# Routing of three chunks placed between attention heads, and the second attention placed between the last gate products

## The reference

```
x += tanh(g_xattn[0]) * MHA16(layernorm(x), ctx)      # 16 heads of 8 features, softmax over 256 keys
x += tanh(g_ffn[0])   * refine(layernorm(x))          # "experts of a controller", below
x += tanh(g_xattn[1]) * softmax(ln(x) @ ctx.T) @ ctx  # one head over 128 features
x += tanh(g_ffn[1])   * MoE(layernorm(x))             # top 2 of 8 experts, silu(x W1 + b1)*(x W2 + b2) W3 + b3

refine(y): top 2 of 8 experts by a router (gelu hidden layer of 32), their softmax weights w
   twice:  for the shared net and the two chosen experts k:
             a, b, g = split(gelu([s, v] @ W1 + b1) @ W2 + b2)
             v_k = sigmoid(a) * v - softplus(b) * (s - mu);  s_k = s + 0.1 * sigmoid(g) * v_k
           s, v move by halt = sigmoid(...) toward the weighted mean of s_k, v_k
   out = y + integration_weight * (gelu(s @ F1) @ F2)
```

## Time and profile before

| | before |
|---|---|
| median of 3 runs (lowest, highest) | 716.54 us (714.27, 717.22) |
| the profiled execution | 722.34 us, span of the core 720.5 us |
| busy PE / DVE / ACT / POOL | 570.3 / 425.7 / 291.7 / 173.9 us |
| mean granted clock of TensorE | 0.868 of 2.4 GHz |
| setup, to the first exponential | 0 to 63.7 us |
| heads | 63.7 to 198.3 us |
| first routing | 198.3 to 246.4 us |
| first hidden units and first softplus products | 246.4 to 286.9 us |
| gates and second round, up to the last 14 gate products | 286.9 to 443.4 us |
| the last 14 gate products | 443.4 to 478.0 us |
| refine, second attention, second routing, table | 478.0 to 566.8 us |
| shares, biases, wait for the first block | 566.8 to 588.0 us |
| 39 expert blocks | 588.0 to 701.7 us |
| gather and output | 701.7 to 720.5 us |

### The profile page before, as it was taken

One profiled execution on the slowest core, in us unless ns is written; L12 is line 12 of the kernel. 1 busy time (PEld: TensorE's weight loads), 2 busy tenths in 40 slices (PEclk: granted clock), 3 DMA queues, 4 the chain that ended last, 5 costly groups with the idle time before them and its releaser, 6 DMA issues.

```text
span 720.5 us, 9536 instructions
## 1 busy us (share of the span) xinstructions
PE 570.3 (79%) x3162; PEld 340.8 (47%) x3172; DVE 425.7 (59%) x1018; ACT 291.7 (40%) x614; POOL 173.9 (24%) x186
## 2 busy tenths in 40 slices
PE   3526877878876989999999999986864189999990
PEld 2302343333343324444444444444753079999990
DVE  4957678795227475868536666666585224444543
ACT  1603555465444754444444125233521034444440
POOL 2283000010040291000660000003047603333330
PEclk9955698697667999999999999999785559999995
DMA  7598940000079000000000000041001358999966
GB/s 239 148 187 174 181 55 2 2 3 2 1 245 333 3 1 0 0 1 0 0 1 0 0 1 0 0 118 13 1 20 49 96 164 277 328 306 322 326 236 182
DMA packets 53240, 72.36 MB, mean 100 GB/s; under 512 B 11244, under 2 KB 41268, under 8 KB 52772
## 3 DMA queue, kind: packets, MB, share of 16 engines
q1 hardware_dynamic: 50200, 66.81, 33.0%
q0 software_dynamic: 2272, 4.69, 1.8%
q10 hardware_dynamic: 720, 0.27, 0.2%
HBM read 59.59 MB, written 22.08 MB: 113 GB/s over the span
## 4 chain that ended last, share of the span: by engine, by line
PE 55%; DVE 18%; DMA 9%; issue 5%; SPq 4%; ACT 4%; POOL 3%; another core or an unknown queue 2%; ACTq 0%; POOLq 0%; DVEq 0%
PE psum L1412 18%; PE psum L1295 5%; DVE negmax L856 4%; PE psum L1587 4%; PE psum L1282 3%; POOL hidden L604 3%; PE psum L1401 3%; DMA sorted_y<-yb,xb 3%; PE psum L1403 2%; DMA wb<-in_wall_dram 2%; PE psum L1409 2%; PE psum L1598 2%; DMA ks<-stacked 2%; ACT probs L661 1%
## 5 line engine op out<-in xcount | busy, mean ns | idle before, releaser
L1412 PE MATMUL psum<-hidden,ew 128*128 128x512 f32 x320 | 143.8, 592 | 1.8 <-DVE soft L981 0.8
L661 ACT ACTIVATE probs<-psum 128x512 f32<-128x512 f32 x128 | 70.3, 595 | 62.2 <-PE psum L1282 61.4
L856 DVE TENSOR_REDUCE negmax<-psum 128x4 f32<-128x1024 f32 x64 | 76.5, 1217 | 31.9 <-PE psum L1259 31.8
L1412 PEld LDWEIGHTS psum<-hidden,ew 128*128 128x128 f32 x320 | 60.8, 190 | 69.8 <-issue 68.7
L1587 PE MATMUL psum<-xbT,wb 128*128 128x128 f32 x624 | 78.3, 280 | 1.5 <-DMA wb<-in_wall_dram 1.4
L1217 DVE SCALAR_TENSOR_TENSOR gated<-psum,wb,silu_g 128x128 f32<-128x128 f32 x156 | 43.9, 344 | 59.9 <-ACT silu_g L792 53.1
L604 POOL TENSOR_TENSOR hidden<-unmasked,chosen 128x512 f32<-128x512 f32 x32 | 48.7, 1541 | 112.6 <-ACT unmasked L697 111.5
L1587 PEld LDWEIGHTS psum<-xbT,wb 128*128 128x128 f32 x624 | 74.4, 195 | 2.7 <-DMA wb<-in_wall_dram 2.6
L792 ACT ACTIVATE silu_g<-psum,wb 128x128 f32<-128x128 f32 x156 | 44.6, 368 | 59.1 <-PE psum L1587 54.6
L1282 PE MATMUL psum<-qs,ks 50*128 50x256 bf16 x256 | 52.3, 325 | 18.1 <-ACT probs L661 14.5
L1259 PE MATMUL psum<-ks,qs 48*128 48x256 bf16 x256 | 45.0, 338 | 26.0 <-DMA ks<-stacked 14.1
(11 more groups left out here) (221 smaller groups left out, 884.8 us busy)
## 6 DMA issues: line engine op xcount, KB each, us to landing
wb<-in_wall_dram SPq DMA_DIRECT2D x39, 516.0 KB
wb<-in_wall_dram SPq DMA_DIRECT2D x39, 256.0 KB
sorted_x<-in_slots_dram SPq DMA_DIRECT2D x1, 9815.0 KB, 33.1
stacked<-parts SPq DMA_DIRECT2D x8, 384.0 KB, 5.0
qs<-stacked SPq DMA_DIRECT2D x8, 384.0 KB, 7.3
ks<-stacked SPq DMA_DIRECT2D x8, 384.0 KB, 9.1
xb<-sorted_x SPq DMA_DIRECT2D x39, 65.0 KB, 3.3
ctxT<-in_ctxT_dram SPq DMA_DIRECT2D x2, 1024.0 KB, 6.9
```

The costliest lines, as they stand in the source:

```text
L661: nc.scalar.activation(probs[:, g % 2, h % 4, :, :], s2[n % 2].rearrange("p (k q) -> p k q", k=2), ACT.Exp, scale=float(HD) ** -0.5).then_ ...
L856: nc.vector.tensor_reduce(negmax[:, p].rearrange("p h q -> p (h q)"), psum[:, i:i + 2, :].rearrange("p h (q k) -> p (h q) k", q=2), AX.X, ...
L1412: last = nc.tensor.matmul(dst, ew2[:, j, cols], hidden[:, k - 1, j, c, :], start=False, stop=(j == 3))
```

## The change

The heads, their arithmetic and the 39 blocks stay. Seven things are different.

1. **Routing between heads.** The heads run in one loop over n = 16 b + h. Chunk c (0, 1, 2) has its routing in the 32 heads that follow the last head of its two sequences. `wave(n)` gives the place r = 0..31 in it, and `AT` names the places: norm at 8 to 10, `columns` 11, `router` 13, `logits` 15, choice of experts 16, weights 17, `routeT` 18, the eight `chosen` products at 19, 20, 21, 25 to 29, `weight` 30 and 31. All of these use bank 7 in turn, also with the output projection, and `o` has only bank 6. ACT alone keeps all eight `chosen` results and copies both forms of routeT.
2. **Chunk 3's routing** stands between the hidden units of chunks 0 to 2 and the softplus products of chunks 0 and 1. The hidden units of chunk 3 come after the gates of chunks 0 and 1. Each routing step is for one chunk.
3. `unmasked` has four buffers, not two.
4. **Softplus** is max(x, 0) + ln(1 + exp(-|x|)): three ACT functions (Abs from PSUM, Exp, Ln) in place of two, and on DVE one max-and-add and one scaling in place of min, max and scaling.
5. **Sigmoid** becomes Tanh of half the argument, and the factors are folded into the steps.
6. **Tail.** The last 14 gate products (both of chunks 2 and 3, second round) are places t = 0..13 of a loop of 28, in which refine, the second attention and the second routing of chunks 0 to 2 stand at the places of `TAIL_AT`. Chunk 3's begin at t = 14. These steps share banks 0 to 4 in turn, gates keep 5 to 7.
7. Loads: `choice_sel` (256 KB) and `weight_sel` (128 KB) are issued with the other weights before the first `stack_out`. The fill of `sorted_x` (9.8 MB) no longer waits for the end of the heads. `send_rows` and the norms of POOL are in a new written order. PE waits for the table before the shares.

```diff
+WAVE = BC * H
+PROJECT_AFTER = 6
+AT = {"columns": (11,), "router": (13,), "logits": (15,), "routeT": (18,), "chosen": (19, 20, 21, 25, 26, 27, 28, 29), "weight": (30, 31)}
+L = NC - 1
+GATES = 14
+TAIL = 28
+TAIL_AT = {"up": (0, 1, 9, 14), "down": (2, 3, 10, 15), "columns2": (5, 6, 12, 18), "rowsT": (12, 14, 18, 24),
+           "scores": (6, 7, 9, 10, 13, 14, 19, 20), "probsT": (7, 8, 10, 11, 14, 15, 20, 21), "fused": (8, 9, 11, 12, 15, 16, 21, 22),
+           "logits2": (13, 15, 19, 25), "ranks": (14, 16, 20, 26)}
+def wave(n):
+    return [(c, n - WAVE * (c + 1)) for c in range(L) if 0 <= n - WAVE * (c + 1) < WAVE]
...
+            def softplus(m, k):
+                if m >= 2:
+                    act.wait_ge(state_ready, m - 1)
+                u = 3 * m + k
+                act.wait_ge(soft_psum, u + 1)
+                t = soft[:, k, m % 2, :]
+                steps.then(nc.scalar.activation(t, bank[2 + u % 3], ACT.Abs, bias=sb2[:, 1:2] if k == 0 else 0.0))
+                steps.wait()
+                steps.then(nc.scalar.activation(t, t, ACT.Exp, scale=-1.0))
+                steps.wait()
+                nc.scalar.activation(t, t, ACT.Ln, bias=1.0).then_inc(ln_done, 1)
...
+            for n in range(WAVE * NC):
+                b, h = n // H, n % H
+                exps(b, h)
...
+                for c, r in wave(n):
+                    for i in parts_at("columns", r):
+                        copy_columns(c)
+                    for i in parts_at("router", r):
+                        router_gelu(c)
+                    if r == 16:
+                        exp_gap(c)
+                    for i in parts_at("routeT", r):
+                        copy_routes(c)
+                    for i in parts_at("chosen", r):
+                        keep_choice(c, i)
+                    for i in parts_at("weight", r):
+                        keep_weight(c, i)
...
+                for c, r in wave(n):
+                    if r == 8:
+                        first_norm(c)
+                    if r == 10:
+                        first_apply(c)
+                    if r == 16:
+                        choose_experts(c)
+                    if r == 17:
+                        weigh_choices(c)
...
+            for j in range(5):
+                hidden_unit(0, j)
+            project(B - 1)
+            for j in range(5):
+                hidden_unit(1, j)
+            for j in range(3):
+                hidden_unit(2, j)
+            columns(L)
...
+            soft_part(1, 2)
+            for i in range(3, 8):
+                choice(L, i)
+            for k in range(2):
+                choice_weight(L, k)
+            gate_parts(0)
+            gate_parts(1)
+            for j in range(5):
+                hidden_unit(L, j)
...
+            rstd_of_chunk(2, 0)
+            rstd_of_chunk(2, 1)
+            rstd_of_chunk(3, 0)
+            rstd_of_chunk(2, 2)
+            rstd_of_chunk(3, 1)
+            send_rows(0, range(0, GR // 2))
+            rstd_of_chunk(2, 3)
+            send_rows(0, range(GR // 2, GR))
+            rstd_of_chunk(3, 2)
+            send_rows(1, range(0, GR))
+            send_rows(2, range(0, GR // 2))
+            rstd_of_chunk(3, 3)
+            send_rows(2, range(GR // 2, GR))
+            send_rows(3, range(0, GR))
...
+            for t in range(TAIL):
+                if t < GATES:
+                    gate_part(NC + 2 + t // 7, t % 7)
+                for c in tail_at("up", t):
+                    refine_up(c, 0)
+                    refine_up(c, 1)
+                for c in tail_at("down", t):
+                    refine_down(c)
+                for c in tail_at("columns2", t):
+                    columns2(c)
+                for c in tail_at("rowsT", t):
+                    rows_to_columns(c)
+                for b in tail_at("scores", t):
+                    scores(b)
+                for b in tail_at("probsT", t):
+                    transpose_probs(b)
+                for b in tail_at("fused", t):
+                    fuse(b)
+                for c in tail_at("logits2", t):
+                    route_logits(c)
+                for c in tail_at("ranks", t):
+                    route_ranks(c)
```

More of the change, by code:

```diff
@@ new lines, in _, with exps2 @@
+            softplus_of(NC + 3)
+            def exps2(b):
+                act.wait_ge(negmax2_ready, b + 1)
+                if b >= 2:
+                    act.wait_ge(probsT_psum, b - 1)
+                ps = tail_bank("scores", b)
+                for q in range(2):
+                    last = nc.scalar.activation(probs2[:, b % 2, q, :], ps[:, q * S:(q + 1) * S], ACT.Exp,
+                                                bias=negmax2[:, b, q:q + 1], accum_out=sums2[:, b, q:q + 1])
+                last.then_inc(exp2_done, 1)
```

1462 lines of the change are left out of this document (812 added, 650 removed).

## The result

The kernel after takes 739.86 us (median of 4 runs, 734.66 to 742.00) against 716.55 us before: 1.030 times as long (95% interval 1.026 to 1.034). It is slower. The prediction was 694.5 us, with 674 to 718 as its range and 0.12 for slower. The profiled execution took 742.0 us, its span is 740.2 us, so 19.7 us above the 720.5 us of before.

What follows compares the result with a forecast made beforehand. It took the heads as DVE-bound at full clock, PE-bound at half, and later stretches as PE-bound or hand-over chains. Terms +1 + 22 - 39 + 1 - 7 = -22 gave 700.3 us, 694.5 us against the median; range 674 to 718.

Steps and rivals of the forecast that it cites:

- The heads: Heads stage: routing of chunks 0 to 2 placed between heads adds 22 us (+12 to +36).
- The work term: Heads: each chunk's routing adds 7.1 us of PE work at full clock.
- The clock term: Heads: +13 if the clock stays high, +34 if low as often as today; +22 taken between.
- heads of more than 170 us: Named sign, about the clock, that the prediction is wrong; forecast was heads of 134.6 + 22 us.
- Rival (b): Heads pay for the routing in full at 1.2 GHz, 52 us in all, whole 724.5 us; chance 0.12.
- the gelu stall: Heads, in rival (b): ACT's gelu stall costs 3.2 us a chunk.
- Routing of chunk 3: Last head to first gate product takes 44 us; with first softplus and moved hidden products, -39 us (-44 to -30).
- The wait for masks: Before the first gate: third hidden unit waits for POOL's masks, within 6 us shared with the last kept choices and weights.
- Controller: Gate and softplus stage: same PE work, extra ACT pass hidden, +1 us (-3 to +3).
- Tail: Last 14 gate products, refine, second attention and routing up to the blocks: -7 us (-21 to +8).
- unexplained stalls: Tail: waits of 6.4 us behind the table and 4.76 us; half expected to come again, -5 us.
- rival (d): Table switches drain the engine: nine more loads, each with a 1283 ns pause, +12, 706.5 us; chance 0.03.

Runs made afterwards that it cites:

- e17: e6 with the projection at head 4 instead of 6, so TensorE waits for VectorE's normalised values: 752.8 us, heads 158.2 us.
- e2: The kernel after with the whole routing of chunks 0 to 2 moved behind the heads, still one bank for weighed values: 750.4 us, heads 157.8 us.
- e6: e2 with two banks for the weighed values and each group of them one head earlier: 719.4 us, heads 127.7 us.
- e7: e1 with two banks for the weighed values: 724.9 us, heads 165.0 us.
- e1: The kernel after with the chosen and weight products of chunks 0 to 2 moved behind the heads: 727.8 us, heads 166.6 us.
- e13: The kernel after with each product of scores by key done twice in sequences 2 to 7: 749.2 us, heads 212.7 us.
- e14: The kernel after with VectorE's normalisation ahead of the row maxima of head 2 and the transposes of normed rows at place 12, not 11: 739.2 us.
- e3: The kernel after with the router's Gelu of chunks 0 to 2 replaced by an Identity of the same size: 741.6 us, heads 199.0 us.
- e4: e2 with each product of scores by key done twice in sequences 2 to 7: 746.3 us, heads 152.4 us.
- e11: The kernel before with each product of scores by key done twice in sequences 2 to 7: 712.8 us, 0.994 of before.
- e5: e2 with the heads' order of before on TensorE and VectorE, including two banks for weighed values: 729.1 us, heads 132.6 us.
- e16: e9 with the transposes of the normed rows at place 15 instead of 11: 700.4 us, 0.969 of before.
- e9: e6 with transposes of normed rows kept between heads and the remaining routing behind them step by step, in six banks with own buffers: 712.9 us.

## Why the prediction was wrong

**The heads, the step that failed.** The step was "I take +22, between them, since PE is busier but the loop is also slower", with ends that assumed a clock no lower than today's. The work term held: 8.2 us a chunk against 7.1 (the terms that I listed add to 7.9, not 7.1). So did those of DVE and ACT, busy for 101.5 and 107.8 us where I had about 101 and 105. The clock term did not, and the sign that I had named for it, heads of more than 170 us, is what came. The time at 1.2 GHz went from 62.9 of 134.6 us to 127.4 of 199.2. I had taken, a sequence at 2.4 GHz with 3.6 us idle in 14.7, as a stable state to which a load can be added. It isn't: in e17 11.5 us more of waiting make the heads 30.5 us longer. I listed the change of `o` to one bank and the projection's new place among the facts and gave them no price. e2 against e6 puts 30.1 us of heads and 31 us of the whole on them when nothing else is in the heads. In after they aren't separable like that, since e7 beats e1 by only 1.6 us of heads: there, it seems, either cause alone already keeps the clock down. What is shown is that the clock fell and that order and bank alone can do it. Which hand-over of the routing does it in after is open (e13, e14).

**Rival (b) had half of the mechanism.** It had the clock at 1.2 GHz and 52 us for the heads, 724.5 us, and it "decides from 14.7 us per chunk". The heads took 21.5 us a chunk, 64.6 us against the 52 of the rival, because the first two sequences lengthened as well (17.7 and 19.0 us against 16.3 and 17.1), and because of the added waits. The other half of (b), the gelu stall of 3.2 us a chunk, wasn't there (e3), so that it comes near in time is in part luck. My argument against it, that a third more work should lift the clock, is right for work without waits in e4 and e11, and wrong for work that comes with hand-overs (after, e7) and for work without waits among them (e13).

**Routing of chunk 3, right.** 45.0 us against 44 forecast. The wait for masks that I had put at up to 6 us is in the chain, on DVE rather than POOL:

```profile
265.42 5.73 DVE hidden L1173 x4
...
272.87 2.38 DVE hidden L1173 x4
```

**Controller, right within 2 us.** +4.4 us with chunk 3's hidden products, where I had 5.4 and 1.

**Tail, right, with a surprise at its end.** The last gate product ends 64.3 us after the first of the 14, where I had 68.6 (34.6, 27 and 7), and the table comes 56.7 us behind it, where I had 53. Behind the table I counted on half of the unexplained stalls going. The sum took the stall of 4.76 us out twice, once in the 45 and again in the -5; with half of both coming again the tail would have been -3, not -7, against -10.6 measured. What now sets the end there is POOL, but not by the order that I feared: it has nothing to do for 4.6 us ahead of 587.5, then DVE has the places of chunk 3's last rows, and eight scatters run back to back. The last of them lands at 598.8, and the blocks' rows are loaded from there on.

```profile
586.08 1.44 issue
587.51 0.96 POOL sorted_x L738
...
596.49 2.33 DMA sorted_x<-kept,choices
```

The tail's -10.6 us is no accident of one execution: from the start of the last 14 gate products to the first block it is 144.7 us before and 131.9 to 134.7 us in after, e1, e2, e6 and e7.

**The blocks, not predicted.** They and the end give back 4.9 us. PE waits there for the experts' weights 4.3 us in 7 waits, against 1.4 us in 4 before. The same stretch takes 134.8 to 139.5 us in e1, e2, e5, e6 and e7, against 132.4. I looked for no cause of it by a run, so only the wait is shown.

**The changes that wouldn't matter didn't.** Setup 0. The table loads in the heads cost nothing (e3), and behind 21 of the 25 loads of after the next function starts within 0.02 us, so the pause of rival (d) isn't there.

## What to carry to other kernels

When TensorE runs at 2.4 GHz with a quarter of its time idle, don't price a new wait by its length. Here 11.5 us of it made the heads 30.5 us longer (e17), and 4.3 us in longer single waits went with 30.1 us (e2 against e6), so there is no fixed factor either. Look at each place where it would wait on another engine for more than a microsecond: one such place a sequence was worth 33 us, while 18 us of extra products made the kernel before no slower. Before moving work into a stage "with room", run the stage once with only the order and the buffers changed and the work left out, since the order may be the dearer part. And a step belongs as far behind its producer as its buffers allow: four heads later was worth 12.5 us here (e16 against e9).

## What was not expected of the hardware

- Added matmuls made a kernel no slower, and by a little faster: e11 with 18.2 us more work at full speed takes 0.994 (0.991 to 0.998) of before.
- In e17 the clock fell in or just behind five pauses of TensorE of 2.7 us, and stayed at 1.2 GHz for 3.4, 3.4, 10.2, 10.2 and 58 us, although TensorE was busy for 8.7 of the 9.4 us from 165.2 to 174.6.
- The same kernel differs by its clock from one execution to the next: e16 ran in 695.6 us at a mean of 0.899 and in 708.1 us at 0.875.
